# Eight PSUM banks divided anew between two attention passes and the side chunks, with the attention's division done through DRAM

## The reference

```
for i in range(6):
    xn = adaln(x, noise_emb, n1_w[i], n1_b[i])
    q, k, v = split(xn @ qkv_w[i].T);  q, k = rope(q), rope(k)
    x = x + attn(q, k, v, src_mask) @ so_w[i].T
    xn = adaln(x, noise_emb, n2_w[i], n2_b[i])
    q, k, v = rope(xn @ cq_w[i].T), rope(context @ ck_w[i].T), context @ cv_w[i].T
    x = x + attn(q, k, v, ctx_mask) @ co_w[i].T
    xn = adaln(x, noise_emb, n3_w[i], n3_b[i])
    x = x + gelu(xn @ f1_w[i].T + f1_b[i]) @ f2_w[i].T + f2_b[i]
# attn: softmax(q k^T / 4) v per head, scores exact to float32
# then: layernorm, router, top 2 of 8 experts with at most 640 rows each, gelu FFN per expert, weighted sum
```

## Time and profile before

| | us |
|---|---|
| time, median of 3 runs (4446.65 to 4462.31) | 4453.81 |
| the profiled execution's own time | 4442.28 |
| its span in the trace | 4440.6 |
| TensorE busy | 3940.5 (89%) |
| VectorE busy | 2907.1 (65%) |
| ScalarE busy | 2561.9 (58%) |
| GpSimd busy | 857.7 (19%) |

### The profile page before, as it was taken

One profiled execution on the slowest core, in us unless ns is written; L12 is line 12 of the kernel. 1 busy time (PEld: TensorE's weight loads), 2 busy tenths in 40 slices (PEclk: granted clock), 3 DMA queues, 4 the chain that ended last, 5 costly groups with the idle time before them and its releaser, 6 DMA issues. The chain is left out here.

```text
span 4440.6 us, 68492 instructions
## 1 busy us (share of the span) xinstructions
PE 3940.5 (89%) x20630; PEld 1833.7 (41%) x20630; DVE 2907.1 (65%) x4711; ACT 2561.9 (58%) x4302; POOL 857.7 (19%) x518
## 2 busy tenths in 40 slices
PE   3699999999999999999999999999999999997467
PEld 1233344533344533345433345433345433354355
DVE  3777766677766678766678766678766677752311
ACT  1376656667666567666567665567666566654122
POOL 4312121112121112211111211111211121200133
PEclk7799999999999999999999999999999999999689
DMA  5354323244323244332244332244332344410234
GB/s 162 85 135 108 97 69 78 63 108 120 87 78 72 60 113 119 87 80 65 67 108 116 94 72 66 68 108 116 97 75 59 74 129 111 109 30 13 83 99 95
DMA packets 271578, 396.39 MB, mean 89 GB/s; under 512 B 28312, under 2 KB 218400, under 8 KB 270880
## 3 DMA queue, kind: packets, MB, share of 16 engines
q1 hardware_dynamic: 263904, 382.18, 34.1%
q0 software_dynamic: 7296, 9.51, 1.3%
HBM read 226.63 MB, written 170.67 MB: 89 GB/s over the span
## 5 line engine op out<-in xcount | busy, mean ns | idle before, releaser
L837 ACT ACTIVATE prob<-ps 128x512 f32<-128x512 f32 x3072 | 1768.2, 596 | 1225.2 <-PE ps L761 1207.6
L999 DVE TENSOR_REDUCE negmax<-ps 128x2 f32<-128x1024 f32 x1536 | 1836.7, 1219 | 217.6 <-PE ps L788 195.2
L761 PE MATMUL ps<-qstack,kstack 114*128 114x512 bf16 x3072 | 1162.4, 389 | 100.1 <-ACT prob L837 84.8
L774 PE MATMUL psv<-prob,v 128*32 128x512 f32 x6144 | 829.5, 612 | 0.0
L761 PEld LDWEIGHTS ps<-qstack,kstack 114*128 114x128 bf16 x3072 | 284.6, 97 | 1190.3 <-ACT prob L837 794.5
L616 POOL TENSOR_TENSOR rot<-ropep 128x512 f32<-128x512 f32 x96 | 122.5, 1276 | 2486.7 <-DVE ropep L1032 2467.7
L788 PE MATMUL ps<-kstack,qstack 49*128 49x512 bf16 x3072 | 496.8, 388 | 97.9 <-DVE negmax L999 76.8
L736 PE MATMUL side<-anat,wf 128*128 128x256 f32 x1536 | 377.1, 388 | 9.9 <-DVE hT L1037 8.9
L1037 DVE TENSOR_SCALAR hT<-side,f1b 128x256 f32<-128x256 f32 x384 | 168.2, 479 | 303.6 <-PE side L736 303.6
L747 PE MATMUL side<-wf,hT 128*128 128x256 f32 x1536 | 347.9, 379 | 2.8 <-DVE x L1044 1.6
L736 PEld LDWEIGHTS side<-anat,wf 128*128 128x128 f32 x1536 | 285.6, 192 | 65.7 <-DVE hT L1037 30.9
(11 more groups left out here) (158 smaller groups left out, 3722.1 us busy)
## 6 DMA issues: line engine op xcount, KB each, us to landing
bounce<-parts SPq DMA_DIRECT2D x480, 256.0 KB, 2.5
qstack<-bounce SPq DMA_DIRECT2D x384, 192.0 KB, 5.5
kstack<-bounce SPq DMA_DIRECT2D x384, 192.0 KB, 6.1
bounce<-low SPq DMA_DIRECT2D x96, 256.0 KB, 2.1
ctxT<-in_ctxT SPq DMA_DIRECT2D x24, 512.0 KB, 3.9
nw<-in_nwT SPq DMA_DIRECT2D x18, 512.0 KB, 11.3
w<-in_w SPq DMA_DIRECT2D x16, 512.0 KB, 4.8
wself<-in_wself SPq DMA_DIRECT2D x24, 256.0 KB, 4.0
```

The source lines that it names most:

```text
L761: nc.tensor.matmul(ps2[:, n % RING2, :], kk[0:ROWS, h, kt * P:(kt + 1) * P], q[0:ROWS, h, :], start=True, stop=True).then_inc(s_p2full, 1)
L774: mm = nc.tensor.matmul(psv[32 * i:32 * i + 32, 0, :], v[j % 2][:, kt, (HD + 1) * h:(HD + 1) * h + 32], prob[:, 4 * (u % 2) + i, :], start ...
L837: nc.scalar.activation(prob[:, 4 * (u % 2) + i, :], ps2[:, n % RING2, :], ACT.Exp, scale=HD ** -0.5).then_inc(s_prob, 1)
L999: nc.vector.tensor_reduce(out_at, ps1[:, 2 * (n % 2):2 * (n % 2) + 2, :], AX, ALU.max, negate=True).then_inc(s_p1free, 1)
```

## The change

- PSUM: `ps1` goes from 4 banks to 2, `ps2` from 2 to 3, `side` from 1 to 2; `psv` keeps 1. The side chunks alternate between two banks with a semaphore each.
- TensorE's order within a unit: one pass 1 pair at the unit's start, and the second just before the value products.
- T1 and T2 are gone, with their transposes, divisions and copies. Instead SP writes each group of `osum` to DRAM (`value_sums`), loads the row sums into `den` and the 256 rows of values into `aT`; VectorE takes the reciprocal of `den` at place 4; SP writes it to DRAM (`inverse`) and loads it back repeated 16 times into `recips`, which uses the memory of `nT`; GpSimd multiplies `aT` by it as the first thing in its slot.
- The places of the chunks, of the statistics, of the splits and of gelu are other ones. O moves from 19 and 21 to 18 and 20 in a short slot and from 11 and 12 to 8 and 10 in a long one.
- Experts: the transposes are made two parts ahead.

```diff
-RING2 = 2
+RING2 = 3
...
 LONG_PLACES = {
-    "HV": [1, 3], "T1": [2, 4, 5, 7], "HT": [6, 8], "T2": [9, 10], "O": [11, 12], "HQ": [13, 14],
-    "HK": [15, 16], "LT": [17, 18], "F1": [19, 20, 21, 22, 23, 24, 25, 26], "F2": [27, 28, 30, 31],
+    "HV": [1, 3], "HT": [5, 7], "O": [8, 10], "HQ": [9, 11], "HK": [12, 13], "LT": [15, 16],
+    "F1": [17, 18, 19, 20, 21, 22, 23, 24], "F2": [26, 27, 29, 30],
 }
...
-        ps1 = psum("ps1", 4)
+        ps1 = psum("ps1", 2)
...
-        side = psum("side", 1)
+        side = psum("side", 2)
...
+            def write_sums(j, g):
+
+                sp.wait_ge(s_os, place.jobs(j, 4) + g + 1)
+                sp.dma_start(sums[j % 2][4 * g:4 * g + 4].rearrange("h r n -> (h r) n"), osum[:, g, :]).then_inc(s_sums, 16)
+
+            def load_attention(j):
+
+                sp.wait_ge(s_sums, place.jobs(j + 1, 64))
+                sp.dma_start(den[:, :], sums[j % 2][:, HD].rearrange("h (c n) -> h c n", c=P // H)).then_inc(s_den, 16)
+                for k in range(KD):
+                    sp.dma_start(aT[:, k, :], sums[j % 2][8 * k:8 * k + 8, 0:HD]).then_inc(s_aload, 16)
+                sp.wait_ge(s_recip, place.jobs(j + 1, 1))
+                sp.dma_start(inverse[j % 2].rearrange("h (c n) -> (h c) n", c=P // H), recip[:, :]).then_inc(s_inv, 16)
+                sp.wait_ge(s_inv, place.jobs(j + 1, 16))
+                for k in range(KD):
+                    sp.dma_start(recips[:, k, :], inverse[j % 2][8 * k:8 * k + 8, None, :].to_broadcast([8, HD, S])).then_inc(s_aload, 16)
...
             def slot(k, p2, p1, tail, head):
                 side_done = place.at(start[k], CHUNKS_PER_LAYER)
+                if tail:
+
+                    sp.wait_ge(s_full, side_done)
+                    write_sums(k - 2, 3)
+                    load_attention(k - 2)
...
+                if tail:
+                    pool.wait_ge(s_aload, place.jobs(k - 1, 64))
+                    nc.gpsimd.tensor_tensor(aT[:, :, :], aT[:, :, :], recips[:, :, :], ALU.mult).then_inc(s_anorm, 1)
...
+                if what == "O":
                     if c == 0:
-                        wait_read(pe, place, k, "T2", 0)
-                        wait_read(pe, place, k, "T2", 1)
+                        pe.wait_ge(s_anorm, place.jobs(k - 1, 1))
...
-                if j > 0 or n >= 2:
-
-                    pe.wait_ge(s_p1free, place.jobs(j, PAIRS) + n - 1)
+                if j > 0 or n >= 1:
+
+                    pe.wait_ge(s_p1free, place.jobs(j, PAIRS) + n)
...
                 for u in range(SLOT_UNITS):
+                    if p1:
+                        pass1(k, 2 * u)
                     if p2:
                         pass2(k - 1, u, 0)
-                    if p1:
-                        pass1(k, 2 * u)
-                        pass1(k, 2 * u + 1)
-                    if p2:
                         pass2(k - 1, u, 1)
...
                     if p2:
                         pass2(k - 1, u, 2)
+                    if p1:
+                        pass1(k, 2 * u + 1)
                     if u and p2:
                         pv(k - 1, u - 1)
...
+                    if tail and at == RECIP_PLACE:
+                        dve.wait_ge(s_den, place.jobs(k - 1, 16))
+                        nc.vector.reciprocal(recip[:, :], den[:, :]).then_inc(s_recip, 1)
...
+            gather_T(1)
             for n in range(len(PARTS)):
                 if n + 1 < len(PARTS):
-                    gather_T(n + 1)
                     hidden(n + 1)
+                if n + 2 < len(PARTS):
+                    gather_T(n + 2)
                 outputs(n)
```

More of the change, by code:

```diff
@@ L411, in slot_chunks @@
             if tail:
-                put("T1", "T2", "O")
+                put("O")
             if p1:
@@ L438, in wait_read, with bank_of @@
         def wait_read(eng, place, k, what, c):
-            eng.wait_ge(s_read, place.at(number[(k, what, c)] + 1, CHUNKS_PER_LAYER))
+            n = number[(k, what, c)]
+            eng.wait_ge(s_read[n % 2], place.at(n // 2 + 1, CHUNKS_PER_LAYER // 2))
+        def bank_of(k, what, c):
+            n = number[(k, what, c)]
+            return side[:, n % 2, :], s_read[n % 2]
         def cross_before(j):
@@ L865, in modulate @@
                     be = mod[:, bass.ds(i, 1), KD + c, b:b + 1].rearrange("p a b -> p (a b)")
-                nc.scalar.activation((nT if what == "LT" else xnT)[:, c, :], side[:, 0, :], ACT.Identity, scale=g, bias=be).then_inc(s_read, 1)
+                bank, read = bank_of(k, what, c)
+                nc.scalar.activation((nT if what == "LT" else xnT)[:, c, :], bank, ACT.Identity, scale=g, bias=be).then_inc(read, 1)
             def hi(j, w):
@@ L884, in side_work @@
             def side_work(k, what, c):
-                bank = side[:, 0, :]
+                bank, read = bank_of(k, what, c)
                 if what in ("HT", "LT"):
                     modulate(k, what, c)
-                elif what == "T2":
-                    wait_filled(act, place, k, what, c)
-                    nc.scalar.activation(aT[:, c, :], bank, ACT.Copy).then_inc(s_read, 1)
                 elif what == "HV":
@@ L1010, in side_work @@
             def side_work(k, what, c):
[L1011 removed]
+                if what not in ("HQ", "HK", "O", "F1", "F2"):
                     return
                 wait_filled(dve, place, k, what, c)
[L1014 to L1021 removed]
+                bank, read = bank_of(k, what, c)
+                if what in ("HQ", "HK"):
                     j, w = k + 1, int(what == "HK")
```

102 lines of the change are left out of this document (49 added, 53 removed).

## The result

The changed kernel takes **4873.97 us** (median of 4 runs, 4871.23 to 4888.89) against 4454.35 (4 runs) for the kernel before: 1.0949 times as long, 95% interval 1.0919 to 1.0978. The profiled execution spans 4870.6 us, 430 more than before. The direction was forecast, the size was not: 4628 was forecast, 4740 was the upper end.

The account below looks back on a forecast made before the run. Plain units were taken as bound closely by TensorE and VectorE, F1 and F2 by TensorE. Short slots +156, long +25, ends +15, experts -21: +175 on 4442.3 gives 4617, with 11.5 for the median 4628 us; range 4480 to 4740.

Parts of the forecast that it names:

- The round trip: Pass 1 on one pair of banks: pair, maximum, next pair; no half shorter than 1.70 us, a plain unit 3.40 for 2.89.
- my halves: The half-by-half sums of a slot's 32 halves: short slot 71.1 us (+4.7), long slot 93.7 us (-3.5), before DMA waits.
- the 1.8 at the reciprocal: VectorE's wait in half 4 for the sums through DRAM: 1.8 us per slot, 0 to 3.7.
- The Q/K pairs of halves at 6.0 us: Two halves with a Q or K chunk, whose side product, rotation and maximum form a loop: 6.0 us against 4.95.
- O's wait for the path: TensorE at O in half 8 of long slots waits for GpSimd's product: 2.85 us per long slot, 0 to 3.4.
- R: The time the reciprocal can start, forecast 13.3 us after the slot's start, bounds 9.3 to 15.2.
- the 9.5: Time from the reciprocal's start through the inverse's write, two loads and GpSimd's product, until O's input is ready: 9.5 us.
- -3.5 for a long slot without waits: Long slot 93.7 us against 97.2: TensorE-bound stretches lose the transposes and do not feel the round trip.
- Ends and experts: First and last slots together +15 us (5 to 25); eight experts, gathering two parts ahead, -21 us.
- +6.5 us for all 24 short slots: Each short slot 4.7 us longer by its halves plus 1.8 waiting at the reciprocal: +156 us in 24.
- Rival 2: TensorE's clock falls after the wait at O, 4.5 us more in 22 slots: 4727; with h5's wait up to 4835; 12%.
- rival 5: Worse: stack loads delay the DMA path beyond 6 us a step, over 4740 us; chance 7%.

Follow-up runs that it names:

- path_o: DRAM path and new experts on the PSUM banks, order and places of before, reciprocal at half 7; long slots have HQ at 10, 11, O at 12, 13: 4306.7 us, 0.9676.
- places_o: `places_old` with, in long slots, O one half later (12 and 13), the norm's statistics behind it and HQ ahead (10 and 11): 4571.4 us, 1.0271.
- split_earlier: `places_o` with ScalarE's first two splits in short slots one half earlier (12 and 14, not 13 and 15): 4499.2 us, 1.0120.
- both_later: Changed kernel with long slots' O at halves 12 and 13, what follows later, reciprocal at 7 instead of 4, ScalarE's copies waiting for all four writes: 4661.7 us, 1.0468.
- order_alone: Kernel before with only the new order in a unit, pass 1's four banks kept: 4581.7 us, 1.0290.
- clock_kept: Changed kernel with extra, overwritten TensorE products before O's and HT's waits in long slots (five and three): 4864.5 us, 1.0924.
- dram_alone: Kernel before with the division through DRAM, new places and new experts, but PSUM banks and unit order as before: 4698.8 us, 1.0555.
- attention_first: Changed kernel with SP issuing the attention's transfers ahead of the second half's ten stack loads: 4759.5 us, 1.0684.
- psum_alone: Kernel before with the PSUM part only: one pass 1 pair, three pass 2 banks, two side banks, new unit order; T1 and T2 stay: 4527.0 us, 1.0169.
- places_old: Changed kernel with all chunks, splits and norms at the places of the kernel before and the reciprocal at half 7: 4647.0 us, 1.0434.

## Why the forecast was too low

The account of the 420 us between 4454 and 4874, by the runs: experts -22 (4432); the path with O and the reciprocal late enough, places otherwise nearly the old ones, -125 (`path_o`, 4307); the PSUM split and its order at these same places +265 (`places_o`, 4571), of which 72 go where two splits stand one half earlier (`split_earlier`, 4499; that move was not run on the old banks); the other new places +91, of which by the quarters some 64 in long slots (100.2 for 97.3) and 30 in short ones (`both_later`, 4662); the reciprocal at half 4 +56 (4718); O at half 8 +156 (4874). The steps depend on their order, as the split's two prices show.

**The round trip: right in size.** 1.72 us a half against 1.70. Summed from my halves, the quarters of a short slot (with the 1.8 at the reciprocal, where the mean wait is 1.0) are 19.1 + 24.0 + 16.2 + 13.6; measured 19.5 + 24.2 + 16.3 + 15.9. The Q/K pairs of halves at 6.0 us held as well. The cause was told too simply: `order_alone` shows that the order with two pass 2 banks gives the same slow unit without any round trip.

**Short slots: the last quarter, 2.3 us short, 41 us in 18 slots.** I had moved Q, K and their splits, but not what follows: the stack loads 5.6 us later, the shift rows behind them, pass 2's wait for those and the low clock. That the shift rows "are wanted only some 40 us into the slot" looked at the path in front of them and missed what was moved at the slot's end.

**Long slots: the step that failed, 10.2 us each, 224 us.** The step is O's wait for the path, priced at 2.85 us a slot, with nothing for the clock behind it. Forecast 98.3, measured 108.5. First quarter, from my halves 23.2, measured 28.9 (125 us in 22 slots). Of these 5.7 us the low clock is 2.2, by `clock_kept`. The other 3.5, by subtraction, are the path's, which ends too late: in the slot shown (its first quarter is 30.2, above the mean) R is 1.4 later than forecast and O 2.7 later after R. Only part of it shows as waits: in the mean of 22 slots 2.1 at the reciprocal (forecast 1.8) and 4.1 at O (2.85), since VectorE and TensorE come to them later too. The banks have little part in it: in `dram_alone`, with two pairs, the first quarter takes 27.5 us and O waits 4.0. The path was mis-sized in its DMA terms: the ten loads' issue at 6.7 for 5.0, a write at 3.8 for 2.3, and loads at 5.4 for 4.3 (the 9.5 took the low end of my own 3.2 to 4.0). I had put the burst into the first write alone (5.5, measured 5.8) and taken lone transfers for the rest. The second quarter is 2.6 longer than forecast, the last two 1.7; the trace has a second fall of the clock there (0.91 from 1440 to 1458 in the slot above, behind a wait of 3.36 us of pass 1), but no run took it away by itself. The transposes' removal, which I credited in full (-3.5 for a long slot without waits), can't be seen there: `places_o`, where O hardly waits, has 97.3, with other places.

**Ends and experts: right.** The start +15 and slot 48 +3, for +15; experts -25 in the trace and -22 in the run, for -21. Slot 49 gained 12, for 0. One error helped the sum by luck: it counted +6.5 us for all 24 short slots, but the 6 first ones of a layer have 69.7 us before, not 66.4, and by my own halves grow by 3.2. That hid 20 us of the shortfall.

**The rivals.** Rival 2 (12%) had the right mechanism and its price, 4.5 us in 22 slots, was twice what the clock costs. The profiled execution lies 255 us above the 4617 forecast for it, and about half of that, the first quarters of the long slots, is rival 2 and rival 5 (7%) together: the path grows by the DMA terms, and the low clock follows O's wait. The rest lies in the other quarters of the long slots (some 95 us) and in the last of the short ones (41). I had priced the rivals as alternatives, and the range ended where one of them began. The Trainium skill (TensorE: Matmul & The Clock Gate, section HAM oscillation) has a wait that returns in each pass throttle the engine each time; the trace agrees, with 0.50 behind O's wait of 4.82 us, and with 3.4 to 3.8 us for O's eight products in 20 of the 22 long slots. My argument against it, the 1.00 of the earlier trace rows, came from a kernel whose steady slots have no wait of that length. The other row that I took for it, I had misread: it holds no wait of 5 us, but a row of short ones, of which these are two:

```profile
4074.98 0.66 PE L663 MATMUL side<-ident,osum 128*128 128x128 f32 x4 [0.72 <-ACT osum L845]
...
4077.92 0.65 PE L663 MATMUL side<-ident,osum 128*128 128x128 f32 x4 [0.81 <-DVE anat L1019]
```

TensorE does 2.23 us of work in these 5 us, and the fall comes behind them all the same; so the rows show a stretch of little work ahead of a fall, not what one wait does. The Trainium skill's page DMA: Bandwidth & Descriptors, section Anatomy of one DMA, gives about 2.0 us of fixed cost per transfer, for transfers that GpSimd issues, with the time for the bytes on top; here SP issues them. `attention_first` measures 2.0 us for a whole write of 256 KB with nothing ahead, and the changed kernel 5.8 behind the burst. Neither page would have given the sum.

What stays open: why long slots with the single pair have 26.0 us in their second quarter in `places_o` against 23.9 in `psum_alone`, and which of the new places makes up the 64 us in `both_later`'s long slots.

## What to carry to other kernels

A wait that an in-order engine meets costs its length, what the engines behind it lose, and, on TensorE, the slow stretch after it; so give a chain of transfers through DRAM the durations measured behind the traffic that will really be ahead of or beside each of them, and place its reader a half or two late rather than just in time. Here one half, with Q moved ahead, was the difference between 1.2% slower and 3.2% faster. A second pair of banks does not show as work anywhere, but it is the cover for the small delays of the engine that reads it: before giving it up, count those delays, not the mean.

## What the runs showed of the hardware

VectorE's operations on SBUF of 0.17 to 0.19 us take 1.14 to 1.18 us, until GpSimd's float32 instruction beside them ends (`places_old` against `split_earlier`). TensorE's granted clock was 0.50 for the whole 4.7 us of the window behind a single wait of 2.46 us, after 9 us at full clock; without that wait it stayed at 1.00 (`split_earlier`). A write of 256 KB landed in 2.0 us with the queue empty, 5.8 us behind ten stack loads; with the attention's transfers in front and those loads beside them, it took 7.0 us from the issue of the inverse's loads to GpSimd's product, against 5.4. With the mean granted clock and its two levels of 1.2 and 2.4 GHz, TensorE spent (1 - 0.924) x 2 x 4870.6 = 740 us of the changed kernel at the low one, against 337 in the kernel before (0.962).
